# A hybrid attention and expert kernel: four record buffers, another order of the scatters in the drain, and result rows numbered for 2 KB loads

## The chip, the cores and the metric

The kernel runs on one core of a Trainium2 chip. A core has five instruction streams: TensorE (PE in the rows; PEld is its weight load), VectorE (DVE), ScalarE (ACT), GpSimd (POOL) and SyncE (SP), and 16 DMA engines that all of them can feed. The metric is the device time of one execution in microseconds (us); a lower one is better.

## The reference

The input is 16 images of 256 tokens with 128 channels. Three layers follow one another, each added to its input:

```
x = x + window_attention(group_norm(x))      # 16 heads of 32, windows of 64 tokens, position bias, masks
t = t + attention(layer_norm(t))             # 8 heads of 16, over the 256 tokens of an image
t = t + experts(layer_norm(t))               # below
# experts: logits = x @ router_w.T + router_b; the two best of 8 per token, weights = softmax of the two
#   h = x @ fc1_w.T + fc1_b; a = silu(h1) * h2; y = a @ fc2_w.T + fc2_b; out = sum of the two, weighted
```

## The kernel before

**Stages.** The program has three parts. In the first, from the start to about 600 us, the 16 images go through both attentions and the router in one software pipeline. In the second, to about 745 us, 39 tiles of 256 routed tokens go through the experts. In the third, the two results of each token and the residual are added and written out.

**The pipeline.** `iteration(X, G, A, M, Bm, R, L, K)` is written once for each engine and unrolled for i from -2 to 20. Each letter is an image at another stage: group norm (X), first projection (G), window attention (A), the joint between the attentions (M), second attention (Bm), output projection, residual and layer norm (R), router (L), record and slot (K). K runs three images behind Bm, so that in the last passes only the late stages are left; these passes are called the drain here. They are pass 17 (Bm is image 15, R 14, L 13, K 12), pass 18 (R 15, L 14, K 13), pass 19 (L 15, K 14) and pass 20 (K 15). Each pass has eight steps n = 0 to 7. The order of an engine's work is the order of the code; nothing reorders it, and every dependency is a semaphore.

**Routing.** For each token and each of its two experts a record of 130 words is made in `rec`: the normalized token (two copies on POOL, L593), its weight (VectorE, L897 and L900), and the row of the result table `ysl` to which the expert's output goes (POOL, L594, from the constant table `tokid`). Each record is scattered to its slot in the DRAM table `slots` by four indirect DMAs per image, of 128 rows each, which POOL issues (L500). The slot numbers come from a chain over three engines: VectorE picks the two experts (`lg`, `mx`, `ix`, `chose`), POOL adds the two picks (`both`, L551), VectorE adds them to the running count (`ahead`), TensorE counts the tokens ahead of each one in `pM`, VectorE adds the base (`place`, L905), POOL multiplies (`mine`, L545), VectorE sums (`slotf`) and converts (`slot`, L919).

**Buffers.** `rec` and `slot` have two buffers, by the parity of the image. Before POOL copies image j into `rec` it waits until the four scatters of image j-2 have landed (`slot_dma`). An image is scattered one pass after its slots are made: image K-1 in steps 2, 3 and 4 of the pass of K; image 15 in step 6 of its own pass. The copies stand in step 7 of a pass that has Bm, and in step 4 of passes 18 and 19. SyncE zeroes an image's part of `slots` (L420) after the residual of the image before it has been made.

**Unread matmuls.** `keep_awake` (L1168) issues matmuls of 512 columns whose result nothing reads. In passes 17 and 18 there are four at the head of every step. Before the expert tiles 32 more stand at L1445, of 128 columns in float32 (64 matmul records in the trace).

**Experts.** SyncE waits for all scatters to land and loads tile after tile of `slots` (L461). TensorE transposes it (L1413), multiplies (L1420, L1431) and transposes back (L1441). VectorE weighs the rows, and POOL scatters them to `ysl` (L614), one row of 512 bytes per token and expert.

**The end.** SyncE and ScalarE wait for all scatters to `ysl` and issue eight loads each, of 256 KB: `yc[:, 0, g]` for the first expert, `yc[:, 1, g]` for the second, g being a group of 512 tokens. VectorE adds the residual (L1153), POOL adds the two halves (L618), and SyncE writes the group out (L468) from the same queue as its loads. A pair of groups shares one semaphore, so VectorE starts on a group when four loads have landed.

Of the kernel before, what the change touches and what calls it, by code (L numbers as in the profile page):

```python
# [6 lines left out]
B, C = 16, 128  # L7
TOK = 256
NTOK = B * TOK
# [15 lines left out]
ROW = C + 2  # L25
# [11 lines left out]
PTBUFS = 6  # L37
GATHER_AWAKE = 32
# [76 lines left out]
def hybrid_kernel(nc, x_tok, x_ch, w0, wo0, bo0, pos, mask, ident_d, gmat_d, sel_d, iota_d,  # L115
# [5 lines left out]
    with ctx:  # L121
# [43 lines left out]
        rec = sb("rec", [128, 2, 2, 2, ROW])  # L165
# [12 lines left out]
        slot = sb("slot", [128, 2, 2, 2], u32)  # L178
# [140 lines left out]
        slot_dma = sem2("slot_dma")  # L319
# [14 lines left out]
        ysl_v = ysl[0:TOPK * NTOK, :].rearrange("(k g s p) c -> k g p s c", k=TOPK, g=NGRP, p=128)  # L334
# [46 lines left out]
        def _(sp):  # L381
# [73 lines left out]
            for p in range(2):  # L455
                sp.wait_ge(slot_dma[p], 4 * 16 * (B // 2))
# [16 lines left out]
        def _(pool):  # L473
# [13 lines left out]
            def sent(K):  # L487

                return Image(K.j - 1, (K.j - 1) // 2, (K.j - 1) % 2) if K is not None and K.j > 0 else None
# [8 lines left out]
            def scatter(J, s, k):  # L498

                pool.indirect_dma_start(  # L500
                    slots, bass.IndirectOffsetOnAxis(ap=slot[:, J.par, k, s:s + 1], axis=0),
                    rec[:, J.par, s, k, :], None).then_inc(slot_dma[J.par], 16)

            def iteration(X, G, A, M, Bm, R, L, K):
                if X is not None and X.j == GN_FIRST:
                    group_roots(1)
                if X is not None and X.j == 1:
# [4 lines left out]
                    pool.iota(tokid[:, :, :], [[128, 2 * B], [NTOK, 2]], base=0, channel_multiplier=1).then_inc(z_pool, 1)  # L512
# [11 lines left out]
                for n in range(8):  # L524
# [27 lines left out]
                    if n == 2 and sent(K) is not None:  # L552
                        scatter_ready(sent(K))
                    if n == 3 and sent(K) is not None:
                        scatter(sent(K), 0, 1)
                        scatter(sent(K), 1, 0)
# [33 lines left out]
                    if n == (7 if Bm is not None else 4) and L is not None:  # L590

                        for k in range(2):
                            pool.tensor_copy(rec[:, L.par, :, k, 0:C], tn2[:, L.par, :, :])  # L593
                        pool.tensor_copy(rec[:, L.par, :, :, C + 1].bitcast(u32),  # L594
                                         tokid[:, L.j * 2:L.j * 2 + 2, :])\
                            .then_inc(r_two, 1)
                    if n == 2 and sent(K) is not None:
                        scatter(sent(K), 0, 0)
                    if n == (4 if Bm is not None else 3) and sent(K) is not None:
                        scatter(sent(K), 1, 1)  # L600
                    if n == 6 and K is not None and K.j == B - 1:
                        scatter_ready(K)
                        for s in range(2):
                            for k in range(2):
                                scatter(K, s, k)
# [199 lines left out]
        def _(v):  # L805
# [47 lines left out]
            def iteration(X, G, A, M, Bm, R, L, K):  # L853
# [7 lines left out]
                for n in range(8):  # L861
# [32 lines left out]
                    if K is not None and n == 1:  # L894
                        v.wait_ge(q_den, K.j + 1)
                        v.wait_ge(r_two, K.j + 1)
                        v.reciprocal(rec[:, K.par, :, 0, C:C + 1], rden[:, :, :]).then_inc(q_fin, 1)  # L897
                    if K is not None and n == 2:
                        v.wait_ge(q_fin, K.j * 3 + 2)
                        v.tensor_tensor(rec[:, K.par, :, 1, C:C + 1], rec[:, K.par, :, 0, C:C + 1], rexp[:, :, :],  # L900
# [15 lines left out]
                    if K is not None and n == 5:  # L916
                        v.wait_ge(q_fin, K.j * 3 + 3)
                        wait(v, slot_dma[K.par], K.half * 64)
                        v.tensor_copy(slot[:, K.par, :, :], slotf[:, :, :]).then_inc(q_slot, 1)  # L919
# [237 lines left out]
        def _(pe):  # L1157
# [22 lines left out]
            def iteration(X, G, A, M, Bm, R, L, K):  # L1180
# [17 lines left out]
                for n in range(8):  # L1198
# [6 lines left out]
                    elif A is None and R is not None:  # L1205
                        keep_awake(pG, 4)
# [333 lines left out]
```

## Time and profile before

| | us |
|---|---|
| median of three runs | 775.05 (773.21 to 776.81) |
| the profiled execution: its own time | 776.03 |
| the profiled execution: its span, first to last instruction | 774.2 |

Busy time, as a share of the span:

| PE | PEld | DVE | ACT | POOL |
|---|---|---|---|---|
| 84% | 71% | 67% | 65% | 62% |

Two lines of the page show the span in 40 equal slices of 19.4 us, the granted TensorE clock in tenths of full speed and the bytes moved in GB/s:

```profile
PEclk9799999999999999999999999999997789999965
...
GB/s 202 29 3 35 17 21 96 11 91 35 76 98 25 91 42 82 89 34 92 42 82 87 30 97 36 85 83 36 206 122 97 65 43 93 87 88 88 73 137 215
```

The clock has two levels, 1.2 and 2.4 GHz, so a digit between 5 and 9 is a mixture. It is under full speed around the change from the first to the second part (slices 31 and 32) and after the last tile. A share of busy time is a mean over three parts with different limits, so each part is read by itself in the rows below.

### The profile page before, as it was taken

The page shows a single profiled execution, that of the slowest core. Times are in us where ns is not written, and L with a number is a line of the kernel's source. Part 1 is how long each engine was busy: PE and PEld are TensorE (multiplying, and loading weights), DVE is VectorE, ACT ScalarE, POOL GpSimd, SP SyncE. Part 2 cuts the span into 40 slices and gives each one's busy share as a digit, 9 for nine tenths or more (in the row PEclk, how much of TensorE's full clock was granted, in tenths as well). Part 3 has the DMA queues.
Part 4 walks back from the last instruction along what each step waited for, and adds up shares of the span by engine and source line. Part 5 has one row for each costly group of instructions (what it writes and reads, how often), then busy time and mean ns, then how long its engine had stood idle before and what let it go on. Part 6 is the DMA issues. An engine that isn't in the chain of part 4 may idle for free. (4 is left out here: it accounts for less than half of the span.)

```text
span 774.2 us, 20293 instructions
## 1 busy us (share of the span) xinstructions
PE 646.9 (84%) x7070; PEld 546.3 (71%) x7070; DVE 515.2 (67%) x1513; ACT 503.8 (65%) x1427; POOL 483.6 (62%) x556
## 2 busy tenths in 40 slices
PE   3887989998989989899898999978884799999910
PEld 2766877877878778787787877767663688888800
DVE  4666768778787787887878878775342446565512
ACT  2555888778877788877888777765540256666600
POOL 5354656665868677686776767667365336666645
PEclk9799999999999999999999999999997789999965
DMA  7102113032230322303223031230732213233247
GB/s 202 29 3 35 17 21 96 11 91 35 76 98 25 91 42 82 89 34 92 42 82 87 30 97 36 85 83 36 206 122 97 65 43 93 87 88 88 73 137 215
DMA packets 54218, 59.27 MB, mean 77 GB/s; under 512 B 10370, under 2 KB 49410, under 8 KB 53602
## 3 DMA queue, kind: packets, MB, share of 16 engines
q1 hardware_dynamic: 44918, 45.65, 23.0%
q0 software_dynamic: 4544, 9.38, 3.4%
q10 hardware_dynamic: 4656, 2.95, 1.4%
q8 instruction: 57, 0.93, 0.5%
q14 instruction: 43, 0.35, 0.1%
HBM read 36.00 MB, written 28.64 MB: 83 GB/s over the span
## 5 line engine op out<-in xcount | busy, mean ns | idle before, releaser
L566 POOL TENSOR_TENSOR pb<-pb,rcb 128x512 f32<-128x512 f32 x128 | 155.5, 1215 | 151.7 <-DVE rcb L859 150.4
L614 POOL DMA_INDIRECT ysl<-yo,dst x78 | 75.4, 967 | 61.1 <-DVE yo L1133 44.4
L725 ACT ACTIVATE pb<-pSB,mxb 128x256 f32<-128x256 f32 x128 | 59.5, 469 | 46.4 <-DVE mxb L959 45.8
L725 ACT ACTIVATE pb<-pSA,mxb 128x256 f32<-128x256 f32 x128 | 59.6, 475 | 41.2 <-DVE mxb L959 41.2
L574 POOL TENSOR_TENSOR pa<-pa,rca 128x512 f32<-128x512 f32 x64 | 67.2, 1051 | 28.5 <-DVE rca L1024 28.5
L1252 PE MATMUL pTB<-ident,pb 128*128 128x128 f32 x512 | 79.4, 278 | 4.9 <-ACT ptb L739 4.8
L739 ACT ACTIVATE ptb<-pTB 128x512 f32<-128x512 f32 x128 | 77.1, 602 | 1.6 <-PE pTB L1252 1.6
L500 POOL DMA_INDIRECT slots<-rec,slot x64 | 65.3, 1020 | 13.8 <-issue 13.7
L745 ACT ACTIVATE pta<-pTA 128x512 f32<-128x512 f32 x64 | 38.6, 604 | 39.1 <-PE pTA L1344 38.6
L1252 PEld LDWEIGHTS pTB<-ident,pb 128*128 128x128 f32 x512 | 57.4, 141 | 9.0 <-issue 6.6
L959 DVE TENSOR_REDUCE mxb<-pSB 128x2 f32<-128x512 f32 x64 | 43.8, 685 | 20.3 <-PE pSB L1221 20.2
L1307 PE MATMUL pOA<-pta,v 128*64 128x64 f32 x1024 | 44.1, 228 | 13.6 <-DVE t L944 9.0
L1107 DVE COPY xs<-pG 128x256 f32<-128x256 f32 x39 | 16.6, 424 | 57.6 <-PE pG L1413 57.6
L1307 PEld LDWEIGHTS pOA<-pta,v 128*64 128x64 f32 x1024 | 36.0, 138 | 25.4 <-issue 23.4
L1014 DVE TENSOR_REDUCE sma<-pa 128x8 f32<-128x512 f32 x64 | 43.6, 682 | 10.2 <-ACT pa L715 9.3
L1344 PE MATMUL pTA<-ident,pa 128*128 128x128 f32 x256 | 39.6, 278 | 11.7 <-DVE pa L974 8.2
L959 DVE TENSOR_REDUCE mxb<-pSA 128x2 f32<-128x512 f32 x64 | 43.8, 684 | 7.7 <-PE pSA L1221 6.6
L1160 PE MATMUL pG<-xnh,w0h 128*128 128x256 f32 x120 | 40.2, 335 | 8.6 <-ACT v L684 6.5
L770 ACT ACTIVATE ws<-fw 128x773 f32 x39 | 33.0, 848 | 21.8 <-issue 14.5
L684 ACT ACTIVATE v<-pG 64x256 f32<-64x256 f32 x120 | 45.4, 379 | 1.9 <-PE pG L1162 0.9
L1221 PE MATMUL pSB<-kbd,q 128*128 128x256 f32 x256 | 42.6, 289 | 4.7 <-issue 3.4
L1221 PE MATMUL pSA<-kbd,q 128*128 128x256 f32 x256 | 46.1, 303 | 0.0
(221 smaller groups left out, 2015.3 us busy)
## 6 DMA issues: line engine op xcount, KB each, us to landing
slots<-sel_dram SPq DMA_DIRECT2D x16, 1040.0 KB
kbd<-kst SPq DMA_DIRECT2D x128, 64.0 KB, 2.4
xt<-slots SPq DMA_DIRECT2D x39, 130.0 KB, 2.2
xch<-x_ch_dram SPq DMA_DIRECT2D x4, 512.0 KB, 7.0
xt<-x_tok_dram SPq DMA_DIRECT2D x16, 128.0 KB, 2.4
xch<-t SPq DMA_DIRECT2D x16, 128.0 KB, 2.1
fw<-f_dram SPq DMA_DIRECT2D x1, 2048.0 KB
yc<-ysl SPq DMA_DIRECT2D x8, 256.0 KB, 9.4
```

Of the source, the lines that this page charges most:

```text
L500: pool.indirect_dma_start(slots, bass.IndirectOffsetOnAxis(ap=slot[:, J.par, k, s:s + 1], axis=0), rec[:, J.par, s, k, :], None).then_inc( ...
L566: pool.tensor_tensor(pb[:, b, :, :], pb[:, b, :, :], rcb[:, b, :].unsqueeze(2).to_broadcast([128, 2, TOK]), ALU.mult).then_inc(sb_nrm, 1)
L574: pool.tensor_tensor(pa[:, u, :, :], pa[:, u, :, :], rca[:, b, :].unsqueeze(2).to_broadcast([128, 8, WIN]), ALU.mult).then_inc(sa_nrm, 1)
L614: pool.indirect_dma_start(ysl, bass.IndirectOffsetOnAxis(ap=dst[:, t % YB, n:n + 1], axis=0), yo[:, t % YB, n, :], None).then_inc(y_dma[t ...
L684: last = a.activation(v0[WIN * half_:WIN * half_ + WIN, J.par, 2 * pr + w, :, :, half_, :], projection(J, value_use(pr))[WIN * w:WIN * w + ...
L725: last = a.activation(pb[:, b, qc, :], (pSB, pSA)[n % 2][:, qc * TOK:(qc + 1) * TOK], ACT.Exp, bias=mxb[:, b, qc:qc + 1], accum_out=smb[:, ...
L739: a.activation(ptb[:, (J.j * BU + k) % PTBUFS, :, :], pTB[:, :].rearrange("p (a b) -> p a b", a=2), ACT.Copy).then_inc(tb_ev, 1)
L959: v.tensor_reduce(mxb[:, b1, :], bank[:, :].rearrange("p (a k) -> p a k", a=2), AX.X, ALU.max, negate=True).then_inc(sb_max, 1)
L1014: v.tensor_reduce(sma[:, b, :], pa[:, u, :, :], AX.X, ALU.add).then_inc(sa_sum, 1)
L1221: mm = pe.matmul((pSB, pSA)[n % 2][:, qc * TOK:(qc + 1) * TOK], q1[:, Bm.par, n // 4, qc * 128:(qc + 1) * 128], kbd1[Bm.par][:, part, n // ...
L1252: mm = pe.transpose(pTB[:, kc * TOK + qc * 128:kc * TOK + (qc + 1) * 128], pb[:, k % PBUFS, qc, kc * 128:(kc + 1) * 128], ident[:, :])
L1307: mm = pe.matmul(pOA[WIN * jj:WIN * jj + WIN, w * WIN:(w + 1) * WIN], v0[:, J.par, w, jj, u, :, :].rearrange("p a d -> p (a d)"), pta[:, u ...
```

## The change

1. `rec`, `slot` and `slot_dma` get four buffers (`RBUFS = 4`), picked by the image number modulo four. The copies of image j wait for the scatters of image j-4.
2. POOL's scatters are issued by a small table, `departures`. Up to pass 16 it says what stood there before: image K-1 in steps 2, 3 and 4, but the wait for the first one (`scatter_ready`) now stands at the end of step 2. In pass 17 it adds the four scatters of image 12 in steps 6 and 7. In pass 18 image 13 goes in steps 5 and 6. In pass 19 two scatters of image 14 go in step 6, in pass 20 the other two in step 3 and image 15 in step 6.
3. The copies into `rec` stand in step 7 in all passes, the drain included.
4. In pass 18 the four unread matmuls stay in steps 3 and 5 alone: 8 are left of 32.
5. `tokid` numbers the result rows otherwise: the token of group g, quarter s and partition p had the row 512 g + 128 s + p of `ysl`, and now has 512 g + 4 p + s. So the load of a group takes 2 KB in one piece per partition, where it took four pieces of 512 bytes. The output rows are written as before.

```diff
-        rec = sb("rec", [128, 2, 2, 2, ROW])
+        rec = sb("rec", [128, RBUFS, 2, 2, ROW])
...
-        slot_dma = sem2("slot_dma")
+        slot_dma = [sem(f"slot_dma{n}") for n in range(RBUFS)]
...
-        ysl_v = ysl[0:TOPK * NTOK, :].rearrange("(k g s p) c -> k g p s c", k=TOPK, g=NGRP, p=128)
+        ysl_v = ysl[0:TOPK * NTOK, :].rearrange("(k g p s) c -> k g p s c", k=TOPK, g=NGRP, p=128)
...
+            def departures(K, n):
+
+                if K is None:
+                    return []
+                left, one = B - 1 - K.j, ((0, 0), (0, 1), (1, 0), (1, 1))
+                if left == 0:
+                    return {3: [(image(K.j - 1), sk) for sk in one[2:]], 6: [(K, sk) for sk in one]}.get(n, [])
+                if left == 1:
+                    return [(K, sk) for sk in one[:2]] if n == 6 else []
+                if left == 2:
+                    return {5: [(K, sk) for sk in one[:2]], 6: [(K, sk) for sk in one[2:]]}.get(n, [])
+                before = {2: one[:1], 3: one[1:3], 4: one[3:]}.get(n, ()) if K.j > 0 else ()
+                at_once = {6: one[:2], 7: one[2:]}.get(n, ()) if left == 3 else ()
+                return [(image(K.j - 1), sk) for sk in before] + [(K, sk) for sk in at_once]
...
-                    pool.iota(tokid[:, :, :], [[128, 2 * B], [NTOK, 2]], base=0, channel_multiplier=1).then_inc(z_pool, 1)
+                    pool.iota(tokid[:, :, :].rearrange("p (g s) k -> p g s k", s=4), [[GRP, NGRP], [1, 4], [NTOK, 2]], base=0,
+                              channel_multiplier=4).then_inc(z_pool, 1)
...
-                    if n == (7 if Bm is not None else 4) and L is not None:
+                    if n == 7 and L is not None:
...
-                        wait(pool, slot_dma[L.par], L.half * 64)
+                        wait(pool, slot_dma[L.j % RBUFS], L.j // RBUFS * 64)
...
-                    elif A is None and R is not None:
+                    elif A is None and R is not None and (Bm is not None or n in (3, 5)):
                         keep_awake(pG, 4)
```

**POOL in passes 18 to 20.** Before, from pass 18 to the scatters of image 14 (`rs` is the inverse root of image 15's layer norm, `both`, `mine` and the scatters `slots<-rec,slot` are as above; what stands in brackets are the semaphores waited for):

```order
L500 DMA slots<-rec,slot 33024x130 [waits q_w2,q_slot,z_slot0,r_two]
L545 TENSOR_TENSOR mine<-chose,place 128x32 [waits q_fin,q_place]
L500 DMA slots<-rec,slot 33024x130 x3
L593 COPY rec<-tn 128x2x128 [waits slot_dma0,r_tn]
L593 COPY rec<-tn 128x2x128
L594 COPY rec<-tokid 128x4
L541 TENSOR_TENSOR rs<-rs,half 128x2 [waits r_eps]
L551 TENSOR_TENSOR both<-chose 128x16 [waits q_pos,q_a1,q_top]
L500 DMA slots<-rec,slot 33024x130 [waits q_w2,q_slot,z_slot1,r_two]
L545 TENSOR_TENSOR mine<-chose,place 128x32 [waits q_fin,q_place]
L500 DMA slots<-rec,slot 33024x130 x3
L593 COPY rec<-tn 128x2x128 [waits slot_dma1,r_tn]
```

And the same stretch now, from pass 18 to the copies of image 15:

```order
L569 TENSOR_TENSOR mine<-chose,place 128x32 [waits q_fin,q_place]
L523 DMA slots<-rec,slot 33024x130 [waits q_w2,q_slot,z_slot1,r_two]
L523 DMA slots<-rec,slot 33024x130
L565 TENSOR_TENSOR rs<-rs,half 128x2 [waits r_eps]
L575 TENSOR_TENSOR both<-chose 128x16 [waits q_pos,q_a1,q_top]
L523 DMA slots<-rec,slot 33024x130 x2
L614 COPY rec<-tn 128x2x128 [waits slot_dma2,r_tn]
L614 COPY rec<-tn 128x2x128
L615 COPY rec<-tokid 128x4
L569 TENSOR_TENSOR mine<-chose,place 128x32 [waits q_fin,q_place]
L575 TENSOR_TENSOR both<-chose 128x16 [waits q_pos,q_a1,q_top]
L523 DMA slots<-rec,slot 33024x130 [waits q_w2,q_slot,z_slot0,r_two]
```

The copies stood ahead of `rs` and `both` in their pass and now stand behind them; the scatters of an image stand in the pass in which its slots are made.

**TensorE in pass 18.** Before (`pTB` the transposes of image 15's last two heads, `pOB` its attention output, `pOA` first the output projection and then the transposed layer norm):

```order
L1168 MATMUL pG<-w0h 128x512 x4
L1268 MATMUL pOB<-ptb,v 32x256 [waits tb_ev]
L1268 MATMUL pOB<-ptb,v 32x256 x7
L1168 MATMUL pG<-w0h 128x512 x8
L1283 MATMUL pOA<-wo1s,o 128x128 [waits r_f,oa_ev,ob_ev]
L1283 MATMUL pOA<-wo1s,o 128x128 x3
L1168 MATMUL pG<-w0h 128x512 x8
L1358 MATMUL pOA<-ident,tn 128x128 [waits r_tn]
L1358 MATMUL pOA<-ident,tn 128x128
L1168 MATMUL pG<-w0h 128x512 x4
L1384 MATMUL pM<-rws,t2f 128x8 [waits r_f,r_lgev]
```

Now:

```order
L1282 MATMUL pOB<-ptb,v 32x256 [waits tb_ev]
L1282 MATMUL pOB<-ptb,v 32x256 x7
L1182 MATMUL pG<-w0h 128x512 x4
L1297 MATMUL pOA<-wo1s,o 128x128 [waits r_f,oa_ev,ob_ev]
L1297 MATMUL pOA<-wo1s,o 128x128 x3
L1182 MATMUL pG<-w0h 128x512 x4
L1372 MATMUL pOA<-ident,tn 128x128 [waits r_tn]
L1372 MATMUL pOA<-ident,tn 128x128
L1398 MATMUL pM<-rws,t2f 128x8 [waits r_f,r_lgev]
```

Four unread matmuls went from ahead of `pOB`, four of eight from between `pOB` and `pOA`, four of eight from behind `pOA`, and the last four from ahead of the router's logits.

## Rows read from the trace of the kernel before

**Rows 1.** Who waited for whom, POOL: us in total, times, longest.

```profile
POOL rec L593 <- DMA slots<-rec,slot: 4.2, 2, 2.7
```

**Rows 2.** Chain of waits, 600 to 625: start us, us, what.

```profile
607.02 2.29 DMA slots<-rec,slot
...
613.74 2.04 PE pSA L1420 x4
...
623.97 0.86 PE pSA L1420 x4
```

**Rows 3.** POOL, 575 to 600: start, us, instruction, idle before and releaser.

```profile
575.19 1.04 POOL L566 TENSOR_TENSOR pb<-pb,rcb 128x512 f32<-128x512 f32 x1 [2.86 <-DVE rcb L859]
...
585.12 0.72 POOL L541 TENSOR_TENSOR rs<-rs,half 128x2 f32<-128x2 f32 x1
...
595.93 0.74 POOL L593 COPY rec<-tn 128x256 f32<-128x256 f32 x2 [2.70 <-DMA slots<-rec,slot]
...
596.77 0.21 POOL L551 TENSOR_TENSOR both<-chose 128x16 f32<-128x16 f32 x1
...
598.78 0.24 POOL L545 TENSOR_TENSOR mine<-chose,place 128x32 f32<-128x32 f32 x1 [0.63 <-DVE place L905]
599.18 1.01 POOL L500 DMA_INDIRECT slots<-rec,slot  x1 [0.16 <-issue]
```

**Rows 4.** TensorE, 578 to 613, the same columns.

```profile
578.13 1.18 PE L1168 MATMUL pG<-w0h 128*128 128x512 f32 x4
579.24 1.07 PE L1268 MATMUL pOB<-ptb,v 128*32 128x256 f32 x16
580.24 2.11 PE L1168 MATMUL pG<-w0h 128*128 128x512 f32 x8
582.19 1.05 PE L1283 MATMUL pOA<-wo1s,o 128*128 128x128 f32 x8
...
600.02 8.73 PE L1445 MATMUL pOB<-later,ones 128*128 128x128 f32 x64
612.62 0.44 PE L1413 MATMUL pG<-ident,xt 128*128 128x128 f32 x2 [3.87 <-DMA xt<-slots]
```

**Rows 5.** ScalarE, at 580.

```profile
580.46 0.84 ACT L657 ACTIVATE o<-pOB,bv1s 128x256 f32<-128x256 f32 x2 [2.34 <-PE pOB L1268]
```

**Rows 6.** VectorE, 584 to 605.

```profile
584.55 0.17 DVE L1033 TENSOR_SCALAR rs<-mv 128x2 f32<-128x2 f32 x1
...
588.88 0.17 DVE L869 TENSOR_TENSOR lg<-pM,rbs 128x16 f32<-128x16 f32 x1 [1.91 <-PE pM L1398]
...
589.88 0.19 DVE L882 TENSOR_TENSOR chose<-iota,ix 128x32 f32<-128x32 f32 x1
...
604.42 0.18 DVE L1080 TENSOR_SCALAR t_row<-first_row 128x39 int32<-128x39 f32 x1
```

**Rows 7.** SyncE's DMA issues, at 584.

```profile
584.31 0.70 SPq L420 DMA_DIRECT2D slots<-sel_dram  x1
```

**Rows 8.** Stretch: us, busy PE PEld DVE ACT POOL, then clock, DMA share, GB/s.

```profile
613.00:614.00 1.00, 0.32 (x2) 0.29 (x2) 0.81 (x2) 0.00 (x0) 0.00 (x0) 0.54 0.45 111
```

**Rows 9.** The same view, two stretches in which DMA is full.

```profile
553.00:554.00 1.00, 1.00 (x7) 0.95 (x7) 0.42 (x1) 0.18 (x1) 1.00 (x1) 0.50 1.03 403
756.00:757.00 1.00, 0.00 (x0) 0.00 (x0) 0.53 (x1) 0.00 (x0) 0.24 (x1) 0.50 1.17 290
```

**Rows 10.** All engines, 752 to 768.

```profile
752.61 1.29 DVE L1153 TENSOR_TENSOR yc<-yc,xch 128x512 f32<-128x512 f32 x2 [13.62 <-DMA yc<-ysl]
753.39 2.85 POOL L618 TENSOR_TENSOR yc<-yc 128x512 f32<-128x512 f32 x2 [8.87 <-DVE yc L1153]
...
764.34 2.86 POOL L618 TENSOR_TENSOR yc<-yc 128x512 f32<-128x512 f32 x2 [0.63 <-DVE yc L1153]
```

**Rows 11.** The last adds of POOL, ns min/median/max.

```profile
L618 POOL TENSOR_TENSOR yc<-yc x8: 1253/1446/1642, 753.4 to 765.9; 128x512 f32<-128x512 f32 x8
```

**Rows 12.** Page, costliest groups: busy us, mean ns, idle before, releaser.

```profile
L614 POOL DMA_INDIRECT ysl<-yo,dst x78 | 75.4, 967 | 61.1 <-DVE yo L1133 44.4
```

More of the change, by code:

```diff
@@ L37 @@
 PTBUFS = 6
+RBUFS = 4
 GATHER_AWAKE = 32
@@ L177, in hybrid_kernel @@
         slotf = sb("slotf", [128, 2, 2])
[L178 removed]
+        slot = sb("slot", [128, RBUFS, 2, 2], u32)
         o1 = sb("o1", [128, 2, TOK])
@@ L454, in _ @@
             sp.wait_ge(t_drow, 1)
-            for p in range(2):
-                sp.wait_ge(slot_dma[p], 4 * 16 * (B // 2))
+            for p in range(RBUFS):
+                sp.wait_ge(slot_dma[p], 4 * 16 * (B // RBUFS))
             for t in range(NT):
@@ L485, in _, with image, depart @@
             group_roots(0)
-            def sent(K):
-                return Image(K.j - 1, (K.j - 1) // 2, (K.j - 1) % 2) if K is not None and K.j > 0 else None
+            def image(j):
+                return Image(j, j // 2, j % 2)
+            def departures(K, n):
[11 more added lines that the diff above has]
+                return [(image(K.j - 1), sk) for sk in before] + [(K, sk) for sk in at_once]
+            def depart(K, n):
+                for J, (s, k) in departures(K, n):
+                    if (s, k) == (0, 0):
+                        scatter_ready(J)
+                    scatter(J, s, k)
             def scatter_ready(J):
@@ L500, in scatter @@
                 pool.indirect_dma_start(
-                    slots, bass.IndirectOffsetOnAxis(ap=slot[:, J.par, k, s:s + 1], axis=0),
-                    rec[:, J.par, s, k, :], None).then_inc(slot_dma[J.par], 16)
+                    slots, bass.IndirectOffsetOnAxis(ap=slot[:, J.j % RBUFS, k, s:s + 1], axis=0),
+                    rec[:, J.j % RBUFS, s, k, :], None).then_inc(slot_dma[J.j % RBUFS], 16)
             def iteration(X, G, A, M, Bm, R, L, K):
@@ L551, in iteration @@
                         pool.tensor_tensor(both[:, L.par, :, :], chose[:, 0, :, :], chose[:, 1, :, :], ALU.add).then_inc(q_both, 1)
[L552 to L556, printed above, removed]
-                    if n == (7 if Bm is not None else 4) and L is not None:
+                    if n == 3:
+                        depart(K, n)
+                    if n == 7 and L is not None:
                         if L.j == 0:
@@ L589, in iteration @@
                                            ALU.subtract).then_inc(x_l, 1)
-                    if n == (7 if Bm is not None else 4) and L is not None:
+                    if n == 7 and L is not None:
                         for k in range(2):
-                            pool.tensor_copy(rec[:, L.par, :, k, 0:C], tn2[:, L.par, :, :])
-                        pool.tensor_copy(rec[:, L.par, :, :, C + 1].bitcast(u32),
+                            pool.tensor_copy(rec[:, L.j % RBUFS, :, k, 0:C], tn2[:, L.par, :, :])
+                        pool.tensor_copy(rec[:, L.j % RBUFS, :, :, C + 1].bitcast(u32),
                                          tokid[:, L.j * 2:L.j * 2 + 2, :])\
                             .then_inc(r_two, 1)
[L597 to L605, printed above, removed]
+                    if n != 3:
+                        depart(K, n)
             pipeline(iteration)
@@ L917, in iteration @@
                         v.wait_ge(q_fin, K.j * 3 + 3)
-                        wait(v, slot_dma[K.par], K.half * 64)
-                        v.tensor_copy(slot[:, K.par, :, :], slotf[:, :, :]).then_inc(q_slot, 1)
+                        wait(v, slot_dma[K.j % RBUFS], K.j // RBUFS * 64)
+                        v.tensor_copy(slot[:, K.j % RBUFS, :, :], slotf[:, :, :]).then_inc(q_slot, 1)
                     if M is not None and n == 7:
```

4 lines of the change are left out of this document (2 added, 2 removed).

## The prediction, made before the changed kernel had run

> **What bounds the kernel now.** I read the page's lines over time first. They show three parts with different limits: a pipeline of images to about 600 us, expert tiles in which TensorE is busy all the time, and an end in which TensorE does nothing and DMA is full. Then I read the chain of waits. Between 577 and 610 it hardly touches TensorE and runs over POOL's scatters and their landing; its last link there is the landing of image 15's last scatter, 607.02 + 2.29 = 609.31 [rows 2]. The list of who waited for whom has one line on the buffers: POOL's copies into `rec` waited for scatters twice, 4.2 us together [rows 1]. Both waits are in the drain, so in the steady passes four buffers gain nothing. POOL's timeline shows what queues behind them: the inverse root `rs` of image 15 at 585.12, and `both` of image 15 at 596.77, behind a wait of 2.70 [rows 3]. The windows show DMA full at the end, at 290 GB/s [rows 9], and the last rows the two engines that add there [rows 10].
>
> **Part by part: TensorE in pass 18.** The head sum `pOB` started at 579.24, behind four unread matmuls that began at 578.13 [rows 4]. Without them it starts up to 1.1 us earlier; I take 0.9, since it also needs ScalarE's last copy, which I put at the same moment. ScalarE's `o` began 1.22 after `pOB` did [rows 4, 5], so it runs at 579.55 to 580.4. The projection `pOA` had eight unread matmuls ahead of it and came at 582.19 [rows 4]; with four, TensorE is there at 580.3, and `o` releases it at 580.45. That is 1.75 earlier. VectorE's last step before the root ended at 584.55 + 0.17 = 584.72 [rows 6] and so ends at 582.97.
>
> **POOL, to `rs`.** Its last multiply of pass 17 begins at 575.19 and takes 1.04 [rows 3]. POOL was idle for 2.86 before it: two scatters of image 12 fit there. The pace of scatters is (607.02 - 599.18) / 6 = 1.31 us [rows 2, 3]. Behind the multiply stand the copies of image 13, 596.77 - 595.93 = 0.84 [rows 3], to 577.05; two scatters, to about 579.5; `mine`, 0.24, to 579.8; VectorE's slots, some 0.45; two scatters of image 13, 580.4 to 582.7. POOL is then free before `rs` is wanted, by 0.3 us. So `rs` begins at 583.05, where it began at 585.12.
>
> **POOL, to `both` of image 15.** `rs` takes 0.72 and `both` of image 14 0.21, to 584.0. Two scatters end at 586.6, the copies of image 14 at 587.45. VectorE's reciprocal waits for these copies and `lg` of image 15 stands behind it in VectorE's order: it starts at about 587.65, though its logits are there earlier. From `lg` at 588.88 to the end of `chose` at 589.88 + 0.19 is 1.19 [rows 6], so `both` of image 15 begins at 588.95 instead of 596.77: 7.8 earlier.
>
> **From there to the landing.** Now two scatters of image 14 and the copies of image 15 stand ahead of what needs them: 589.3 to 591.6, then to 592.5. Reciprocal, weight and `place` take about 0.45, `mine` 0.24 and its handing over 0.16 (598.78 to 599.18) [rows 3]. Six scatters follow, where seven did: the first at 593.4, the last at 593.4 + 5 x 1.31 = 599.95, landed 2.29 later, at 602.25. Against 609.31 that is **-7.0 us**. From below this term is bounded by the two waits alone, -4.2 [rows 1], if the order brought nothing; from above by the 7.8 of `both`.
>
> **What could be late in its place.** The table of tiles was ready at 604.42 + 0.18 [rows 6], 5.8 after `mine` of image 15 (598.78). `mine` now comes at 593.0, the table at 598.85, before the landing. The zeros of image 15 were issued at 584.31 [rows 7], after its residual, and now at about 582.6. Its first scatter comes at 593.4 + 2 x 1.31 = 596.0, 13.4 us later; at the 403 GB/s of a full stretch [rows 9] 1,040 KB are 2.6 us, and it would take five times that to hold the scatter. In the steady passes the wait for the slots has moved behind a multiply that POOL does anyway: nothing. `tokid` is one instruction of the start: nothing. The tile loop is the same instructions, and TensorE sets its pace: nothing.
>
> **The clock at the first tiles.** The 32 wide matmuls ended at 600.02 + 8.73 = 608.75, TensorE was idle for 3.87 [rows 4], and at 613 the granted clock fell to half (0.54 in that microsecond, so 1.2 GHz instead of 2.4) [rows 8]. The first group of four matmuls took 2.04, one at the upper level 0.86 [rows 2]. Four groups came before the clock was back: at most 4.7 us lost, some 4.3 by my estimate. Now the matmuls end some 5.8 earlier, at 602.95, and the tokens arrive 7.0 earlier, at 605.6: 2.65 of idleness. Whether the clock falls then, no row says. I take the same loss, gain 0, and keep the 4.3 as a rival.
>
> **The end.** VectorE began at 752.61, when four loads (1.05 MB) had landed; POOL added from 753.39 to 764.34 + 2.86 = 767.20 [rows 10]. In the full stretch of the 2 KB weight loads DMA moved 403 GB/s, in that of the 512 byte pieces 290 [rows 9]. So four loads take 2.6 us, not 3.6: I take 0.9 off, POOL begins at 752.5. All loads (4.19 MB) take 10.4 us instead of 14.5, so POOL no longer waits for any: its waits were 13.81 less four pairs of 2.86 (2.85 for the first), 2.4 us. But its adds took 1.25 us at least and 1.64 at most [rows 11]. I read the long ones as those beside VectorE's add: of each pair, VectorE's second add fell on POOL's first. With the data early, seven of VectorE's eight adds fall on POOL's: 8 x 1.25 + 7 x 0.39 = 12.7, to 765.2; at the old mix 11.4, to 763.9. So -2.0 to -3.3; I take **-2.2**, near the first. What follows the last add is unchanged.
>
> The Trainium skill says in "SBUF — State Buffer" (SBUF: two separate sides) that a VectorE operation with two SBUF inputs and a GpSimd operation that reads SBUF lock each other out for whole instructions. That agrees with the two lengths of the rows; by it the end is worth the smaller of the two gains, without it the larger. The same page of the Trainium skill (Summary: rules for kernel authors) says to reckon with about 358 GB/s between HBM and SBUF; the trace's 403 is above it. By 358 the loads would take an estimated 11.7 us and the end would give 0.3 less.
>
> **The sum.** -7.0 - 2.2 = -9.2. Against the profiled execution's own 776.03 (span 774.2) that is 766.8; that execution lay 0.98 over the median of 775.05, which gives **765.8** for a median.
>
> **Rivals.**
> - **The clock stays up in the first tiles.** For it: the idle gap shrinks from 3.87 to about 2.65. Against it: fewer unread matmuls, and a gap that is still long. 765.8 - 4.3 = 761.5.
> - **The loads are not faster.** The row of 403 is one load of weights into another buffer, and the table's rows were just written. Then the end gives 0: 768.0.
> - **The drain gives half.** POOL is ready for `rs` by only 0.3, and two scatters stand ahead of the last copies; if zeros or slower scatters hold POOL, -3.5 is left: 769.3.
> - **Slower: the rows of `ysl` are spread.** A quarter's tokens now lie 2 KB apart, so the 128 rows of one scatter go over four times the range. If writing them slowed the scatters, the tile loop would pay 39 times. POOL is busy 75.4 us in them and idle 61.1 [rows 12], 1.6 a tile, so each scatter (967 ns) would have to grow by 0.8 before a tile gets longer at all. It cancels the gain at 0.24 us more a tile, and at 0.35 more the kernel is at 779.4. Nothing in the trace speaks for it but that it has not been tried.
>
> **Chances.** Forecast 0.53 (763.5 to 768), clock up 0.22, loads no faster 0.11, half the drain 0.08, slower 0.03, and 0.03 for no change to speak of. The range goes from half a microsecond under the first rival to the third: 760.8 to 769.5. A change under 0.5% (3.9 us) can't be told from none here. All cases but the last two are beyond that: faster 0.93, same 0.04, slower 0.03.
>
> **What would show it.** Right: no wait of `rec` for a scatter's landing; `pOA` near 580.4, `rs` near 583, `both` of image 15 near 589 and the last scatter issued near 600; TensorE's first transposed tokens near 605.6; 400 GB/s or so after the last tile, and POOL's eight adds without a pause, most of them over 1.4 us. Wrong: a wait for the zeros' semaphore ahead of a scatter; POOL's adds still pausing for loads, which says the rate is no better; a first tile group of 0.9 instead of 2.0, which says the clock stayed; a tile period above that of before.

## The result and the profile after

| | before | after |
|---|---|---|
| median, us | 775.05 (769.44 to 776.81, 11 runs) | 767.78 (766.48 to 771.85, 11 runs) |
| ratio to before, with its 95% interval | 1 | 0.9934 [0.9914, 0.9954] |
| profiled execution: own time, span | 776.03, 774.2 | 770.44, 768.6 |

The kernel became faster, by 7.3 us in the medians, 5.6 in the profiled executions and 5.1 (3.6 to 6.7) by the ratio in the table, where 9.2 had been forecast. The time lies inside the range, but that is in part luck: its place there is the sum of misses with both signs. To take them apart, the two traces are cut at six events. The first is the start of POOL's `rs` of image 14 (569.70 before, 571.27 after), called the anchor from here on: up to it the code in front of the drain is the same in every kernel.

| stretch | before | after | difference | forecast |
|---|---|---|---|---|
| start to the anchor | 569.70 | 571.27 | +1.57 | 0 |
| anchor to the last landing in `slots` | 39.61 | 36.13 | -3.48 | -7.0 |
| landing to the first product `pOB` of the tiles | 13.25 | 10.84 | -2.41 | 0 |
| first product to the last scatter of the tiles | 120.99 | 120.62 | -0.37 | 0 |
| issue of the last loads to POOL's last add | 21.30 | 19.74 | -1.56 | -2.2 |
| behind the last add | 7.00 | 7.67 | +0.67 | 0 |

(Between the last scatter of the tiles and the issue of the last loads lie 2.35 before and 2.33 after.)

POOL in the kernel after, 581 to 606 (start us, us, instruction, idle before and releaser), the lines that answer to [rows 3]:

```profile
581.46 0.25 POOL L569 TENSOR_TENSOR mine<-chose,place 128x32 f32<-128x32 f32 x1 [0.40 <-DVE place L919]
583.12 1.01 POOL L523 DMA_INDIRECT slots<-rec,slot  x1 [1.42 <-DVE slot L933]
584.43 0.97 POOL L523 DMA_INDIRECT slots<-rec,slot  x1 [0.30 <-issue]
587.58 0.72 POOL L565 TENSOR_TENSOR rs<-rs,half 128x2 f32<-128x2 f32 x1 [2.17 <-DVE rs L1047]
...
593.35 0.22 POOL L575 TENSOR_TENSOR both<-chose 128x16 f32<-128x16 f32 x1 [0.61 <-DVE chose L896]
594.17 1.03 POOL L523 DMA_INDIRECT slots<-rec,slot  x1 [0.59 <-issue]
...
604.95 0.97 POOL L523 DMA_INDIRECT slots<-rec,slot  x1 [0.30 <-issue]
```

The waits for `rec`, 4.2 us [rows 1], are gone, and `both` of image 15 comes 3.4 us earlier by the trace's own time, 5.0 measured from the anchor. But `rs` waits 2.17 us for VectorE, where the forecast had POOL ready with 0.3 to spare. The reader who follows that wait back comes to TensorE. Its rows in the kernel after, which answer to [rows 4] and in its last line to [rows 2]:

```profile
578.42 1.00 PE L1266 MATMUL pTB<-ident,pb 128*128 128x128 f32 x4 [0.78 <-ACT ptb L753]
...
580.87 1.94 PE L1282 MATMUL pOB<-ptb,v 128*32 128x256 f32 x16
582.73 2.08 PE L1182 MATMUL pG<-w0h 128*128 128x512 f32 x4
584.60 1.42 PE L1297 MATMUL pOA<-wo1s,o 128*128 128x128 f32 x8
...
599.22 8.92 PE L1459 MATMUL pOB<-later,ones 128*128 128x128 f32 x64
610.88 0.44 PE L1427 MATMUL pG<-ident,xt 128*128 128x128 f32 x2 [2.74 <-DMA xt<-slots]
612.00 1.40 PE L1434 MATMUL pSA<-xs,ws 128*128 128x256 f32 x4 [0.68 <-DVE xs L1121]
```

The same 16 matmuls of `pOB` that took 1.07 before take 1.94, and four unread ones take 2.08, not 1.18 [rows 4]. The windows of the same trace say why (stretch, us, busy PE PEld DVE ACT POOL, granted clock, DMA share, GB/s); the last two lines lie in the tiles and in the end, beside [rows 8, 9]:

```profile
576.00:577.00 1.00, 0.00 (x0) 0.02 (x1) 0.41 (x3) 0.86 (x3) 0.64 (x2) 1.00 0.26 87
...
578.00:579.00 1.00, 0.58 (x4) 0.61 (x5) 0.17 (x1) 0.27 (x1) 0.84 (x4) 0.77 0.00 0
...
580.00:581.00 1.00, 1.00 (x9) 0.96 (x12) 0.00 (x0) 0.05 (x1) 0.91 (x1) 0.50 0.20 67
...
616.00:617.00 1.00, 0.79 (x4) 0.74 (x5) 0.85 (x3) 0.35 (x1) 0.00 (x0) 0.96 0.01 2
...
748.00:749.00 1.00, 0.00 (x0) 0.00 (x0) 0.43 (x1) 0.00 (x0) 1.00 (x1) 0.50 1.04 399
```

The same microsecond in the kernel before, where it lies between `pOB` and `pOA`:

```profile
580.00:581.00 1.00, 1.00 (x11) 0.67 (x4) 0.00 (x0) 0.54 (x2) 0.70 (x2) 1.00 0.19 67
```

Without the unread matmuls of steps 0 to 2 TensorE stood still for 1.98 us before 577.01, the whole of the microsecond at 576 included, and for 0.78 before 578.42. At 578 the granted clock fell from 1.00 to 0.50, that is from 2.4 to 1.2 GHz, and stayed there to 585, beside everything on which `pOA` of image 15 depends.

The end of the kernel after, all engines, answers to [rows 10]; the lengths of the single adds (ns, least, median, most) to [rows 11]:

```profile
747.14 1.29 DVE L1167 TENSOR_TENSOR yc<-yc,xch 128x512 f32<-128x512 f32 x2 [12.84 <-DMA yc<-ysl]
747.92 2.85 POOL L632 TENSOR_TENSOR yc<-yc 128x512 f32<-128x512 f32 x2 [8.09 <-DVE yc L1167]
...
751.40 9.53 POOL L632 TENSOR_TENSOR yc<-yc 128x512 f32<-128x512 f32 x6 [0.63 <-DVE yc L1167]
```

```profile
L632 POOL TENSOR_TENSOR yc<-yc x8: 1255/1674/1706, 747.9 to 759.7; 128x512 f32<-128x512 f32 x8
...
L1167 DVE TENSOR_TENSOR yc<-yc,xch x8: 679/1060/1743, 747.1 to 756.8; 128x512 f32<-128x512 f32 x8
```

The loads run at 399 GB/s, not 290, and POOL pauses once instead of before each pair. In return the median of its adds grew from 1446 to 1674 ns.

### The profile page after: what moved, and what is told of

Same layout as the page of the kernel before. It is cut to its first block and busy times, and to the rows that moved or that the text cites. A ratio compares the mean times of both kernels' runs of the same rounds, so it can differ in the third digit from the quotient of the medians.

```text
span 768.6 us, 20244 instructions
## 1 busy us (share of the span) xinstructions
PE 643.4 (84%) x7046; PEld 543.4 (71%) x7046; DVE 518.1 (67%) x1513; ACT 503.8 (66%) x1427; POOL 485.9 (63%) x556
## 3 DMA queue, kind: packets, MB, share of 16 engines
q10 hardware_dynamic: 1584, 2.95, 1.0%
## 5 line engine op out<-in xcount | busy, mean ns | idle before, releaser
L1016 DVE TENSOR_TENSOR pa<-pa,mxa 128x512 f32<-128x512 f32 x64 | 45.0, 703 | 0.3
```

## The experiments

All numbers of a trace are counted from the anchor of that trace, unless a row is shown. "t" is VectorE's start on the last projection of image 15 (`t<-pOA`), which needs `pOA`; "landing" is the end of the last landing in `slots`; the fourth column runs from TensorE's start on the first tokens (`pG<-ident,xt`) to the first product `pOB` of the tiles. Where the code up to the landing is that of before, three executions gave a landing at 39.61, 39.57 and 39.52 (and e2, which differs up to there only in a constant table, 39.84); where it is that of after, 36.13, 37.00 and 35.84. Each kernel was profiled once, so a difference of some tenths in one column shows little.

| kernel | t | landing | tokens to first product | last add to end | ratio to before |
|---|---|---|---|---|---|
| before | 13.59 | 39.61 | 9.94 | 7.00 | 1 |
| after | 14.79 | 36.13 | 7.36 | 7.67 | 0.9934 [0.9914, 0.9954] |
| e1 | 13.58 | 34.82 | 8.96 | 7.69 | 0.9885 [0.9853, 0.9918] |
| e2 | 13.59 | 39.84 | 8.80 | 7.00 | 0.9955 [0.9935, 0.9975] |
| e3 | 13.60 | 36.61 | 8.82 | 7.66 | 0.9966 [0.9948, 0.9983] |
| e4 | 14.79 | 41.22 | 7.50 | 7.03 | 1.0017 [0.9997, 1.0038] |
| e5 | 11.83 | 33.39 | 7.68 | 7.66 | 0.9899 [0.9876, 0.9921] |
| e6 | 13.58 | 32.85 | 8.97 | 7.64 | 0.9870 [0.9845, 0.9895] |
| e7 | 14.60 | not read | 6.01 | 7.68 | 0.9930 [0.9907, 0.9952] |
| e8 | 15.74 | 37.00 | 6.08 | 3.64 | 0.9838 [0.9810, 0.9866] |
| e11 | 11.81 | not read | 6.01 | 3.52 | 0.9780 [0.9748, 0.9811] |

### e1: the unread matmuls of pass 18 back

```diff
-                    elif A is None and R is not None and (Bm is not None or n in (3, 5)):
+                    elif A is None and R is not None:
```

> The changed kernel with all 32 unread matmuls of pass 18 back. In the trace of the changed kernel the granted clock fell to 0.50 at 578.8, in pass 18, and image 15's residual t came 14.8 us after POOL's rs of image 14; before it was 13.6 at clock 1.00. Theory A (the missing matmuls let the clock fall, which cost more than they took): clock 1.00 to the end of pass 18, t again 13.6 after that rs, and the landing of the last scatter about 34.9 after it instead of 36.1; 1.2 us faster than the changed kernel, if the first tiles are alike. Rival F (the fall was chance, and the matmuls are only time on the way): t at 13.6 too, but the changed kernel's other trimmed version (the one with only the trim) shows clock 1.00 and t at 11.9, and this kernel is 1.7 us slower than it would be trimmed.

Measured: 767.04 (762.13 to 768.49). TensorE in e1, start, us, instruction:

```profile
578.45 1.07 PE L1282 MATMUL pOB<-ptb,v 128*32 128x256 f32 x16
579.45 2.13 PE L1182 MATMUL pG<-w0h 128*128 128x512 f32 x8
581.42 1.05 PE L1297 MATMUL pOA<-wo1s,o 128*128 128x128 f32 x8
```

The granted clock is 1.00 until 588, behind the last of these matmuls, `pOB` takes 1.07 again, t is 13.58 and the landing comes at 34.82, 1.3 before that of after. So work that nothing reads made the drain shorter: the drop of the clock costs more than the unread matmuls themselves. The fall was not chance. The seven kernels with all 32 (before, e1, e2, e3, e6, e9, e12) have t at 13.58 to 13.60; in the five with 8 (after, e4, e7, e8, e10) `pOB` took 1.94 each time and t lies at 14.60 to 15.74.

The kernel as a whole gains little by it: the clock at the first tiles, which came back later here than in after (8.96 from the tokens to the first product, 7.36 in after), takes it back. The first product comes at 47.02 from the anchor in e1 and at 46.97 in after.

### e2: only the numbering of the result rows

```diff
-        ysl_v = ysl[0:TOPK * NTOK, :].rearrange("(k g s p) c -> k g p s c", k=TOPK, g=NGRP, p=128)
+        ysl_v = ysl[0:TOPK * NTOK, :].rearrange("(k g p s) c -> k g p s c", k=TOPK, g=NGRP, p=128)
```

(with the constant table `tokid` as in the change)

> The kernel before with the new row numbers alone (2 KB loads). Theory: the drain and the tiles are as before, the loads run at about 400 GB/s, and from the issue of the first load to the end of POOL's last add it takes 19.7 us instead of 21.3: 1.6 us faster than before (0.2%). Rival (the loads' gain is swallowed by POOL's adds getting longer): 0.5 us or less. Rival (the spread rows of ysl slow the scatters): a tile period over 3.08 us and the kernel slower than before.

Measured: 772.07. The end in e2, POOL:

```profile
757.20 6.20 POOL L619 TENSOR_TENSOR yc<-yc 128x512 f32<-128x512 f32 x4 [0.63 <-DVE yc L1154]
```

From the issue of the loads to the last add took 19.59 instead of 21.30, so the renumbering alone is worth 1.7 in this trace. Over all traces with POOL's adds that stretch took 19.59 to 20.21 with the new rows and 21.19 to 21.46 with the old ones, so 1.0 to 1.9. The time of e2 fell by more, since the first tiles were 1.1 shorter too (8.80 instead of 9.94); the renumbering does not touch them. The stretch of the tiles was 120.6 to 120.8 in every kernel with spread rows and 120.6 to 121.0 in those with the old ones: the scatters to `ysl` did not grow, and the rival that forecast a slower kernel falls.

### e3: only the four buffers

```diff
+RBUFS = 4
-        rec = sb("rec", [128, 2, 2, 2, ROW])
+        rec = sb("rec", [128, RBUFS, 2, 2, ROW])
-                        wait(pool, slot_dma[L.par], L.half * 64)
+                        wait(pool, slot_dma[L.j % RBUFS], L.j // RBUFS * 64)
```

(`slot` and `slot_dma` likewise; order of POOL as before)

> The kernel before with four record buffers alone; the order of POOL and the unread matmuls stay. Theory: both waits of the copies for a landing go (1.53 and 2.70 us idle), the 0.3 between the copies and the rs behind them too, so the last scatter lands about 4 us earlier against POOL's rs of image 14: 35.5 instead of 39.6, 4 us faster than before. Then the new order adds little to nothing. Rival (the scatters in front of the copies fill POOL, and the order is what matters): 1.5 us or less.

Measured: 771.62. POOL in e3:

```profile
584.29 0.75 POOL L594 COPY rec<-tn 128x256 f32<-128x256 f32 x2
...
586.35 0.72 POOL L542 TENSOR_TENSOR rs<-rs,half 128x2 f32<-128x2 f32 x1 [1.19 <-DVE rs L1034]
```

No copy waits for a landing, and the landing comes 3.0 earlier, not 4.2: 1.19 of the first wait turned into a wait for VectorE, before `rs`. The new order on top of the buffers, at full clock, brought 36.61 - 34.82 = 1.8 more (e1 against e3).

### e4: only the fewer unread matmuls

The condition of e1's diff put into the kernel before.

> The kernel before with the trim of the unread matmuls in pass 18 alone (8 left of 32). Theory A: the granted clock falls to 0.50 in pass 18 and t comes some 14.8 us after POOL's rs of image 14 instead of 13.6, and since POOL's copies and waits stand there anyway the kernel is 0 to 1.2 us slower than before. Rival F (chance): clock 1.00, t at 11.9, and the kernel as before within 0.5, because POOL's wait for the landing hides what TensorE gives.

Measured: 775.59. TensorE and the windows of e4:

```profile
579.61 1.94 PE L1268 MATMUL pOB<-ptb,v 128*32 128x256 f32 x16
```

```profile
580.00:581.00 1.00, 1.00 (x16) 0.40 (x8) 0.96 (x12) 0.00 (x0) 0.64 (x2) 0.50 0.00 0
```

The same fall to 0.50 and the same 1.94, without buffers or a new order: t is 14.79 as in after, and the landing 1.6 later than before. The tiles get that back (7.50 instead of 9.94), and the time is that of before. Why the clock comes back sooner in the tiles with fewer unread matmuls in pass 18, no run settles.

### e5: unread matmuls in steps 0, 1, 3 and 5

```diff
-                    elif A is None and R is not None and (Bm is not None or n in (3, 5)):
+                    elif A is None and R is not None and (Bm is not None or n in (0, 1, 3, 5)):
```

> The changed kernel with 16 of the 32 unread matmuls of pass 18, those of steps 0, 1, 3 and 5: the ones of steps 0 and 1 lie where TensorE waits for ScalarE's copies anyway. Theory A: with TensorE busy over those gaps the granted clock stays at 1.00, and then what the prediction said of TensorE comes true: t 11.9 us after POOL's rs of image 14 (14.8 in the changed kernel, 13.6 with all 32), rs of image 15 at 13.4, landing at about 33.1 instead of 36.1: 3 us faster than the changed kernel. Rival (any matmul less lets the clock fall): t at 14 or later.

Measured: 765.83. TensorE in e5:

```profile
581.31 1.07 PE L1282 MATMUL pOB<-ptb,v 128*32 128x256 f32 x16
582.32 1.20 PE L1182 MATMUL pG<-w0h 128*128 128x512 f32 x4
583.42 1.16 PE L1297 MATMUL pOA<-wo1s,o 128*128 128x128 f32 x8
```

This separates the two effects of the removed matmuls. Those of steps 0 and 1 hold the clock at 1.00; those of steps 2 and 4 only stand in the way. With the former kept and the latter gone, t is 11.83: 1.76 before that of before, where the prediction had put 1.75. Its arithmetic for TensorE was right for a clock that stays up. That for POOL was not: `rs` came at 13.64, not at 13.35, and here it is POOL that is late. VectorE's part was ready at 586.05, POOL's scatter ended at 586.41:

```profile
582.63 0.26 POOL L569 TENSOR_TENSOR mine<-chose,place 128x32 f32<-128x32 f32 x1
584.12 1.01 POOL L523 DMA_INDIRECT slots<-rec,slot  x1 [1.23 <-DVE slot L933]
585.44 0.97 POOL L523 DMA_INDIRECT slots<-rec,slot  x1 [0.30 <-issue]
586.43 0.73 POOL L565 TENSOR_TENSOR rs<-rs,half 128x2 f32<-128x2 f32 x1
```

From the start of `mine` to the scatter it takes 1.49, where the prediction had 0.84 (579.56 to 580.4). So with the clock held the landing is at 33.39; the forecast was 32.55.

### e6: the copies in step 4 again, at full clock

```diff
-                    if n == 7 and L is not None:
+                    if n == (7 if Bm is not None else 4) and L is not None:
```

(both places, on top of e1)

> The changed kernel with the 32 unread matmuls and with POOL's copies of passes 18 and 19 in step 4 again (four buffers stay, so they wait for no landing). Theory P (the copies of images 14 and 15 hold VectorE's reciprocal and all that stands behind it, and this is the gain that the new order gives back): both of image 15 at 20.3 after POOL's rs of image 14 (20.9 with the copies in step 7), the last landing at about 32.7 instead of 34.8: 2 us faster than the version with the 32 matmuls alone. Rival (POOL's scatters fill the time anyway): the landing at 34.8.

Measured: 764.12. POOL in e6:

```profile
580.79 0.73 POOL L614 COPY rec<-tn 128x256 f32<-128x256 f32 x2
...
582.36 1.02 POOL L523 DMA_INDIRECT slots<-rec,slot  x1 [0.71 <-POOL rec L615]
```

The copies run before `rs` is there, and VectorE's reciprocal no longer holds `lg` of image 15: `both` at 20.33 instead of 20.87. The copies of image 15 stand ahead of its `both` as well, so they are out of the way behind it, where the other 1.4 come from (12.52 from `both` to the landing, 13.95 in e1). The landing is at 32.85, 2.0 before that of e1. So a part of the change, copies late in the drain, works against it once there are four buffers.

### e7: 46 wide unread matmuls before the tiles

```diff
-GATHER_AWAKE = 32
+GATHER_AWAKE = 46
```

> The changed kernel with 46 instead of 32 unread matmuls ahead of the expert tiles. They end just as the first tokens land. Theory C (the gap of 2.7 us lets the clock fall at the first tiles): clock 1.00 from there on, first group of four at 0.9 instead of 1.40, and from the landed tokens to the first projected product about 6.0 us instead of 7.4; 1.3 us faster than the changed kernel. Rival (the clock falls all the same, since TensorE waits for VectorE and ScalarE in the first tiles): no change within 0.5.

Measured: 767.87, against 767.78 of after. TensorE in e7:

```profile
596.39 12.48 PE L1459 MATMUL pOB<-later,ones 128*128 128x128 f32 x92
608.71 0.38 PE L1427 MATMUL pG<-ident,xt 128*128 128x128 f32 x2
```

TensorE does not go idle, the clock stays at 1.00 and the first product follows the tokens by 6.01, the floor without any drop. But the 92 records end at 608.87, about 0.7 after the tokens (an estimate: in after the tokens follow the start of the last scatter by 5.93, which would be 39.41 here, and they start at 40.08), and the first product is at 46.09 from the anchor, 46.97 in after. These 0.9 do not show in the median; in the traces 0.4 of them go again at the end (20.15 from the issue of the loads to the last add, 19.74 in after).

### e8: all adds of the end on VectorE

```diff
-                pool.wait_ge(o_one, g + 1)
-                pool.tensor_tensor(yc[:, 0, g, :], yc[:, 0, g, :], yc[:, 1, g, :], ALU.add).then_inc(o_two, 1)
+                v.wait_ge(o_one, g + 1)
+                v.tensor_tensor(yc[:, 0, g, :], yc[:, 0, g, :], yc[:, 1, g, :], ALU.add).then_inc(o_two, 1)
```

> The changed kernel with both adds of the end on VectorE, none on POOL. In the changed kernel POOL's eight adds took 1.25 to 1.71 us and VectorE's up to 1.74, and both were longest while the other one added. Theory L (they keep each other out): VectorE's 16 adds take 0.68 to 0.70 each, and from the first load's issue to the last add it takes 16.5 to 17.5 us instead of 19.7: 2.5 us faster than the changed kernel. Rival (the loads and writes that go on make the adds slow): VectorE's adds still over 1 us, and no gain.

Measured: 761.67 (759.07 to 763.12). VectorE in e8:

```profile
745.10 0.69 DVE L1164 TENSOR_TENSOR yc<-yc,xch 128x512 f32<-128x512 f32 x1 [12.83 <-DMA yc<-ysl]
...
755.57 0.69 DVE L1166 TENSOR_TENSOR yc<-yc 128x512 f32<-128x512 f32 x1
```

All sixteen adds take 0.69, and issue to last add is 17.10 instead of 19.74. VectorE alone is faster than both together: beside it POOL's add took up to 1.71 and VectorE's up to 1.74. The rest, 4.0, came from behind the last add, 3.64 instead of 7.67. L122 stands for the instructions at the very end of the program, where SyncE waits for the other engines. Its wait, and POOL's closing instruction there (DRAIN; length in ns three times, then its start), in after:

```profile
SPq L122 <- PEq L122: 5.1, 1, 5.1
...
L122 POOLq DRAIN  x1: 9737/9737/9737, 758.6 to 758.6; - x1
```

And in e8:

```profile
SPq L122 <- PEq L122: 0.2, 1, 0.2
...
L122 POOLq DRAIN  x1: 11967/11967/11967, 733.3 to 733.3; - x1
```

In after this DRAIN begins with POOL's last adds and ends at 768.3, 0.3 before the program does. In e8, where POOL has nothing to do after its last scatter, it is over at 745.3, long before the last add.

### e9, e12: what the 0.66 behind the last add is not

e9 adds to the kernel before two semaphores that nothing uses; e12 gives `rec` and `slot` the room of four buffers and uses two.

```diff
+        idle_sems = [sem(f"idle{n}") for n in range(2)]
```

```diff
-        rec = sb("rec", [128, 2, 2, 2, ROW])
+        rec = sb("rec", [128, 4, 2, 2, ROW])
```

> The kernel before with two more semaphores that nothing uses. From the end of POOL's last add to the end of the span it took 7.00 us in the kernel before (and in its versions with the row numbers or the trim alone), and 7.66 in every version with four buffers, which has two more semaphores. Theory S (the end of the program deals with every semaphore on the way out): 7.66 here. Rival (it is the buffers' place in memory or the second pair of waits on SyncE): 7.00.

> The kernel before with the room of four record and slot buffers in SBUF, of which it uses two as before, with its two semaphores. Two more semaphores that nothing uses left the time behind POOL's last add at 6.98 us. Theory R (where the tensors lie decides over the 0.66 us): 7.66 here. Rival (it is the use of four semaphores): 7.00 here, as before.

Measured (single times): 773.65 and 775.38; behind the last add 6.98 and 7.04, as in before. Neither makes the 7.64 to 7.69 that all kernels with four buffers and POOL's adds show (after, e1, e3, e5, e6, e7). The traces say where the difference lies. POOL's DRAIN at the end, in e12:

```profile
L121 POOLq DRAIN  x1: 9083/9083/9083, 764.3 to 764.3; - x1
```

It takes 9.08 or 9.09 in the five kernels with two buffers and POOL's adds (before, e2, e4, e9, e12) and 9.74 in the six with four: these 0.65 are the whole difference. Two more semaphores in use, with the waits on them, remain, alone or together with the room; what in them makes the DRAIN longer is open.

### e10: e8 with the old row numbers

e8 with the lines that e2 removes.

> The changed kernel with both adds on VectorE and the old row numbers (512 byte pieces). Theory: with adds of 0.69 the loads set the end, so what the 2 KB pieces are worth shows in full: at 290 GB/s the last pair lands 17.3 us after the first issue as it did before, and from the issue to the last add it takes about 20 us, against 17.1 with the 2 KB pieces: 3 us, where behind POOL's adds it was 1.6. Rival (the pieces' size matters only a little): under 18.

Measured (a single time): 763.62. Issue to last add is 20.00, against 17.10 in e8. So the renumbering is worth 2.9 when the adds are fast and 1.6 behind POOL's (21.30 and 19.74): nearly half of its gain had been hidden by the adds. The windows of e10, in the loads:

```profile
750.00:751.00 1.00, 0.00 (x0) 0.00 (x0) 1.00 (x2) 0.00 (x0) 0.00 (x0) 0.50 1.22 290
```

### e11: all together

After, with steps 0, 1, 3 and 5 (e5), the copies in step 4 (e6), 42 wide unread matmuls, and VectorE's adds (e8).

> The changed kernel with what the other runs point to: the unread matmuls of pass 18 in steps 0, 1, 3 and 5, POOL's copies of passes 18 and 19 in step 4, 42 unread matmuls ahead of the tiles, both adds on VectorE. By the sum of the parts: t at 11.8 after POOL's rs of image 14 and both of image 15 at 18.8, the landing at 31.3 (changed kernel 36.1), the first product 6.2 after the tokens instead of 7.4, the end 6.6 shorter (2.6 of it adds, 4.0 behind them): 12 us faster than the changed kernel, a median near 755. Rival (POOL becomes the bound in pass 18, since its scatters of image 13 are not out when rs of image 15 is wanted): the landing not before 32.5.

Measured: 756.43 (754.09 to 758.03), 2.2% under before and, by the medians, 1.5% under after. TensorE and POOL in e11:

```profile
592.78 12.10 PE L1458 MATMUL pOB<-later,ones 128*128 128x128 f32 x84
604.72 0.38 PE L1426 MATMUL pG<-ident,xt 128*128 128x128 f32 x2
```

```profile
587.30 0.25 POOL L569 TENSOR_TENSOR mine<-chose,place 128x32 f32<-128x32 f32 x1 [1.48 <-DVE place L916]
```

The matmuls end as the tokens arrive, and the clock stays up in the tiles. It came out 1.4 above what was expected. `both` of image 15 is at 19.86, not 18.8, and the gains of e5 and e6 don't add up in full, for two reasons that the trace shows. `rs` comes at 13.92, again behind POOL's scatters, as the rival had it. And `mine` waits 1.48 (0.77 in e6), because the clock falls once more, at 584, with the router's matmuls behind it:

```profile
584.92 1.00 PE L1397 MATMUL pM<-rws,t2f 128*128 128x8 f32 x4 [0.57 <-ACT t2f L718]
```

The granted clock is 0.67 in the microsecond at 584 and 0.50 in the next. The same four took 0.58 in e5 at clock 1.00.

## Why the prediction was right in direction and wrong in its terms

- **`pOA` 1.75 earlier: this step failed.** The prediction took the unread matmuls for time on TensorE's path and nothing else. The forecast had t 1.75 earlier, and it came 1.20 later. The fall of the granted clock at 578 is the cause: e1 (clock 1.00, t 13.58), e4 (fall and 14.79 by this edit alone) and e5 (clock kept, 11.83) show it. The prediction asked whether the clock would fall at the first tiles, and not in pass 18. The Trainium skill says in "TensorE: Matmul & The Clock Gate" (The HAM clock gate) that the slow level is the default and activity lifts it. These runs agree: the unread matmuls of steps 0 and 1 were what held it (1.00 in e5 with them, 0.50 in after without).
- **`rs` of image 15.** Forecast 2.07 earlier, measured 0.89 later, the same miss carried on (2.95 and 2.96).
- **`rs` to `both`: right.** Forecast 5.9, measured 5.77 (before 11.65). The waits are gone and `lg` follows the copies.
- **`both` to the landing.** Forecast 13.3, measured 14.05. Of the 0.75 that are missing, 0.5 are the first scatter of image 14 behind fresh slots: 0.82 from the start of `both` to it, where the prediction had 0.35. The last scatter landed 2.45 after its issue, not 2.29. VectorE in the kernel after:

```profile
593.19 0.16 DVE L933 CAST slot<-slotf 128x4 uint32<-128x4 f32 x1
```

  The conversion ends at 593.35 and the scatter begins at 594.17. The prediction had charged nothing there. Its row for `mine` to scatter was 0.16 [rows 3], but there the slots had been ready. The same omission made POOL late for `rs` in e5.
- **The drain together**: +2.96 - 0.1 + 0.75 = 3.6 less gain than -7.0 (measured -3.48). The rival "the drain gives half" had the size, by another mechanism: it had POOL late for `rs`, and POOL waited 2.17 there. Only with the clock held (e5) is POOL late, by 0.36. e6 adds that even the mechanism of the forecast stood in the wrong place: copies in step 4 are better by 2.0.
- **The clock at the first tiles: this term was mis-sized too.** Taken as 0 and, as a rival, as 4.3; the kernel before lost 3.9 there (9.94 less the 6.01 of e7 and e11). It fell again but came back at 616, where at 619.26 a group took 0.86 and before only at 623.97 [rows 2]. That gave 2.4, a little over half of the rival. How much it gives is not set by the code alone, nor by the idle gap alone. e8 and e10 are the same as after up to there and had 6.08 and 7.34; e8 kept the clock at 1.00 with TensorE idle for 2.12 ahead of the tokens, and e9 lost it with 2.32 and had 9.95. The same page of the Trainium skill says that at a kernel's start the number of slow matmuls differs between runs of one kernel; here, in its middle, the 6.08 against 7.36 agrees. Only e7 and e11 have no idle gap, and the floor of 6.01. What decides in the others stays open.
- **The end.** First pair 0.76 earlier (forecast 0.9); adds 12.38 (forecast 12.7, by seven pairs that collide); one pause of 0.63 stayed: -1.56 for -2.2. "What follows the last add is unchanged" was wrong by 0.67, with a cause that is only narrowed: it lies in POOL's DRAIN at the end (e3, e9, e12).
- **The start, +1.57.** Code up to the anchor differs only in buffer numbers, one wait and the constant table. Over the traces the anchor lies at 567.58 to 570.50 with two buffers (five) and at 568.50 to 572.79 with four (nine). These overlap, so it is put down to the executions; a small cost of the change in the steady part can't be excluded.

In sum, by stretch: 3.6 too much for the drain, 2.4 too little for the clock at the tiles, 0.6 and 0.7 too much for the end, 0.4 too little for the tiles (in the scatter of this stretch between kernels with the same code): 2.1 above the forecast, and the start's 1.57 makes the 3.6 by which the profiled executions miss it. The median misses by 2.0 only, since the profiled execution of after lay 2.7 above its median, that of before 1.0.

## What to carry to other kernels

Before unread matmuls are removed, find every stretch in which they alone fill TensorE's gaps, read the granted clock there, and price what follows at the lower level: here those of steps 0 and 1 were worth 3.0 us (`t` 14.79 against 11.83), while those of steps 2 and 4 cost 1.75. Then read what follows as well: e1 gained 1.3 at the landing and had none of it left at the first product. When a stage gets its data sooner, look at what two engines do to each other in it; here one engine doing all sixteen adds beat two by 2.6 us. When a stall is gone, try the order of the work around it anew: here copies that had been moved behind other work, to let that go first, were better put back (e6).

## What the runs showed of the hardware

- DMAs are issued by SyncE, ScalarE and POOL in this kernel; no trace here shows one from TensorE or VectorE, so that all five streams can feed the DMA engines is not shown.
- A scatter whose slot numbers VectorE has just converted starts 0.80 to 0.82 us after that conversion ends (after: 582.31 to 583.12 and 593.35 to 594.17; e1: 579.43 to 580.24; e6: 591.13 to 591.94); with slots long ready it follows POOL's last instruction by 0.16 to 0.31.
- Adds of 128x512 in float32 with all operands in SBUF: POOL 1.25 alone and up to 1.71 beside VectorE's, VectorE 0.68 alone and up to 1.74 beside POOL's. With data early, POOL's median became 1.67. This agrees with the lock that the prediction took from the Trainium skill ("SBUF — State Buffer", two separate sides); the runs show besides that it cost more here than the second engine brought.
- The program ends 7.0 to 7.7 us after the last add if POOL did it, and 3.5 to 3.6 after it if VectorE did (e8, e10, e11). POOL's DRAIN at the end of the program takes 9.1 to 12.0 us, and only in the latter is it over before the last add.
